# Masked projections of a four-layer kernel: the low half of the weights is multiplied with the high half of the activations only, in 64-row matmuls behind the whole matmuls of four groups

## The reference, cut to what matters

```python
xn = layernorm(gn(x), norm_w, norm_b)
left  = (xn @ w_left ) * m * sigmoid(xn @ w_lgate)   # m: mask of the token, layers 0 and 2
right = (xn @ w_right) * m * sigmoid(xn @ w_rgate)
out = einsum('bikh,bjkh->bijh', left, right)         # layer 0; the others alike
x = x + (layernorm(out, onorm_w, onorm_b) * sigmoid(xn @ w_ogate)) @ w_out
```

## Time and profile before

| | |
|---|---|
| median of 3 runs | 2098.76 us (2098.36 to 2103.34) |
| profiled execution, its own time | 2098.03 us |
| its span, first to last instruction | 2096.1 us |
| mean granted TensorE clock | 0.962 |
| busy: TensorE, VectorE, ScalarE, GpSimd | 90%, 81%, 76%, 29% |

### The profile page before, as it was taken

One profiled execution on the slowest core, in us unless ns is written; L12 is line 12 of the kernel. 1 busy time (PEld: TensorE's weight loads), 2 busy tenths in 40 slices (PEclk: granted clock), 3 DMA queues, 4 the chain that ended last, 5 costly groups with the idle time before them and its releaser, 6 DMA issues. The chain is left out here.

```text
span 2096.1 us, 44730 instructions
## 1 busy us (share of the span) xinstructions
PE 1876.4 (90%) x14492; PEld 1270.1 (61%) x14492; DVE 1687.9 (81%) x2690; ACT 1587.1 (76%) x2204; POOL 599.5 (29%) x574
## 2 busy tenths in 40 slices
PE   5698979789888999989989899999997889999998
PEld 4423959555422778865632598987552258877665
DVE  6799989989689868778959997978776987777654
ACT  3598969769899647658989885876888976666676
POOL 0001918265200000016500380742870000000755
PEclk8899989999999999999999999999999999999999
DMA  9599938289789838269969965927997994844997
GB/s 395 208 303 316 252 81 232 78 308 368 300 266 335 295 120 291 72 241 389 418 240 317 298 192 151 277 55 282 396 405 255 310 328 158 276 158 164 337 346 277
DMA packets 297397, 549.53 MB, mean 262 GB/s; under 512 B 14768, under 2 KB 170416, under 8 KB 273712
## 3 DMA queue, kind: packets, MB, share of 16 engines
q1 hardware_dynamic: 295680, 538.38, 74.3%
q10 hardware_dynamic: 1584, 9.51, 1.1%
HBM read 371.67 MB, written 176.16 MB: 261 GB/s over the span
## 5 line engine op out<-in xcount | busy, mean ns | idle before, releaser
L1609 POOL TENSOR_TENSOR LR<-LR,sum 128x2048 f32<-128x2048 f32 x30 | 136.6, 4553 | 513.2 <-DVE LR L1422 513.2
L1618 POOL TENSOR_TENSOR LR<-LR 128x512 f32<-128x512 f32 x96 | 140.6, 1483 | 482.4 <-DVE LR L1664 482.2
L677 PE MATMUL bank<-LR,kst 128*128 128x512 f32 x512 | 255.1, 621 | 8.5 <-ACT LR L699 6.3
L877 POOL TENSOR_TENSOR msgs<-sigs,mask_sb 128x256 f32<-128x256 f32 x192 | 129.8, 691 | 463.8 <-ACT sigs L851 460.4
L1512 PEld LDWEIGHTS bank<-kst,LR 128*128 128x128 f32 x1024 | 151.0, 192 | 109.7 <-issue 90.7
L1524 PE MATMUL bank<-LR,wog 128*128 128x512 f16 x768 | 211.7, 385 | 4.7 <-ACT msgs L1565 3.9
L677 PEld LDWEIGHTS bank<-LR,kst 128*128 128x128 f32 x512 | 88.1, 192 | 180.1 <-issue 173.7
L1019 PE MATMUL bank<-LR 128*128 128x256 f32 x768 | 170.9, 384 | 7.0 <-DVE LR L916 4.2
L1277 PE MATMUL bank<-LR 128*128 128x256 f32 x768 | 166.6, 379 | 7.0 <-DVE LR L916 4.2
L1512 PE MATMUL bank<-kst,LR 128*128 128x128 f32 x1024 | 159.4, 279 | 13.9 <-ACT sigs L1560 7.7
L1019 PEld LDWEIGHTS bank<-LR 128*128 128x128 f32 x768 | 147.4, 193 | 27.7 <-DVE LR L916 4.6
(11 more groups left out here) (227 smaller groups left out, 4800.5 us busy)
## 6 DMA issues: line engine op xcount, KB each, us to landing
LR<-XT SPq DMA_DIRECT2D x89, 1024.0 KB, 8.5
XT<-LR SPq DMA_DIRECT2D x47, 1024.0 KB, 8.8
kept<-XH SPq DMA_DIRECT2D x64, 512.0 KB, 5.7
LR<-XH SPq DMA_DIRECT2D x64, 512.0 KB, 6.8
kept<-XHA SPq DMA_DIRECT2D x64, 512.0 KB, 5.2
LR<-XHA SPq DMA_DIRECT2D x64, 512.0 KB, 5.9
OS<-kept SPq DMA_DIRECT2D x12, 2048.0 KB, 8.3
LR<-OS SPq DMA_DIRECT2D x48, 512.0 KB, 8.7
```

Source lines behind the costliest of these rows:

```text
L677: last = pe.matmul(banks[3][:, u * BANK:(u + 1) * BANK], K(K_MEAN), sq[t % 3][:, u * BANK:(u + 1) * BANK], start=True, stop=True)
L1609: pool.tensor_tensor(v, v, token(sum2, c, C), ALU.mult).then_inc(normalized.s, 1)
L1618: pool.tensor_tensor(by_b(x_of(c), q) if end else by_token_cols(x_of(c), q), by_token(gated[t % 4]), by_token_cols(xi[c % len(xi)], q), AL ...
```

## The change

`where` now gives groups in the order of `q` with the two sides next to each other, instead of all of side 0 and then all of side 1. A half of a chunk (four groups, `two` = 0 or 1) first gets its 16 whole matmuls with `whigh`, each group behind its own wait for a free bank. Then come its 16 `wlow` matmuls over 64 rows, alternating between the sides. The first two groups of the half are signalled at the end of the first eight of these, and the other two at the end of the last eight. The product of the low weights with the low activations is no longer formed. Every other engine keeps its code.

```diff
             def where(n, g):
-                return g // 4, 16 * n + 4 * (g % 4)
+                return g % 2, 16 * n + 4 * (g // 2)
...
                         if masked:
-                            for g in range(8):
-                                if g % 2 == 0:
-                                    norm_left(h, g // 2)
-                                pe.wait_ge(products_ready.s, products_ready.n + 32 * i + 8 * h + g - 7)
-                                for j in range(4):
-                                    for part, w in enumerate((whigh, wlow)):
-                                        last = pe.matmul(bank(g)[:, j * P:(j + 1) * P],
-                                                         tokens(h, g // 4, g % 4, j, slice(0, P)),
-                                                         w[:, half * P:(half + 1) * P], start=part == 0, stop=part == 1)
-                                last.then_inc(projected.s, 1)
+                            for two in range(2):
+                                for g in range(4 * two, 4 * two + 4):
+                                    if g % 2 == 0:
+                                        norm_left(h, g // 2)
+                                    pe.wait_ge(products_ready.s, products_ready.n + 32 * i + 8 * h + g - 7)
+                                    for j in range(4):
+                                        pe.matmul(bank(g)[:, j * P:(j + 1) * P],
+                                                  tokens(h, g % 2, g // 2, j, slice(0, P)),
+                                                  whigh[:, half * P:(half + 1) * P], start=j == 0, stop=False)
+                                for q in (2 * two, 2 * two + 1):
+                                    for s, j in sides_last:
+                                        rows = slice(C * s, C * s + C)
+                                        last = pe.matmul(bank(2 * q + s)[:, j * P:(j + 1) * P], tokens(h, s, q, j, rows),
+                                                         wlow[rows, half * P:(half + 1) * P], start=False, stop=j == 3)
+                                        if j == 3:
+                                            last.then_inc(projected.s, 1)
```

## The result

The changed kernel is slower. The first four runs gave a median of 2129.11 us (2121.01 to 2129.31), against 2099.61 for the kernel before: ratio 1.0117, interval 1.0098 to 1.0136. I had forecast 2110 us and a range up to 2125. The direction and the mechanism held; the size did not. A second series of the same kernel, next to 17 runs of the kernel before, gave 2120.83 us (2119.01 to 2124.76) against 2100.89, ratio 1.0095 with interval 1.0076 to 1.0113. So the change cost 29.5 us in the first series, outside my range, and 19.9 us in the second, inside it. The forecast of 10.8 us was about a half of the smaller of the two.

A forecast was written before the change was run, and what follows sets the result against it. TensorE's matmuls bound the kernel at 4.01 us per chunk; a 4.17 us ring would replace them. The four projections' +1.8, +4.7, +1.8 and +2.5 sum to +10.8 us, 2098.8 to about 2110, range 2100 to 2125.

The forecast's parts named there:

- the ring: Masked projections: each half-chunk passes TensorE, ScalarE, GpSimd and VectorE once per chunk without a buffer, 4.17 us against 4.01.
- TensorE's work on a chunk: Masked projections: whole and 64-row matmuls plus switches take TensorE 3.36 us per chunk, down 0.63.
- the floor of 3.80 us: Masked projections: VectorE needs 1.90 us per half-chunk, 3.80 per chunk, as read after a table load.
- the pairs that start together: 64-row matmuls of the two sides start together, a pair costing 0.055 us in layers without mask, taken as 0.062 here.
- steps 2 to 4 of the ring: From first whole matmul to sigmoid: whole matmuls 0.19, switch to narrow ones 0.15, first narrow start to sigmoid 0.47 us.
- step 2: On TensorE: four whole matmuls, first to last start, 3 x 0.0624 = 0.19 us.
- step 4: TensorE to ScalarE: first narrow matmul start to the sigmoid, 0.44 us plus 0.03 for strided tokens, 0.47 us.
- step 1: VectorE to TensorE: from group 3's product taken to the first whole matmul of that bank, 0.06 us.
- Step 5: ScalarE, GpSimd, VectorE: sigmoid of group 0 to the end of group 3's product, 3.30 us.
- the first rival: Masked projections: TensorE's relief counts, each chunk falls to VectorE's 3.80 us, giving 2089 us; chance 0.08.
- The rival of a clock that falls in the projections: TensorE's gaps lower its clock, TensorE's part of the turn grows by about 0.6 us, giving 2145 us; chance 0.02.
- the longer figure: Port wait of VectorE's mask to the end of GpSimd's record: 0.26 instead of 0.13 us, 4.30 us per chunk.

The follow-up runs named there:

- the order alone: Changed kernel with its second pass over all 128 rows again, so only the new matmul order stays: 2125.99 us, ratio 1.0111 to the kernel before.
- a ring over two banks: Changed kernel with the 64-row matmuls behind two groups' whole matmuls instead of four: 2113.42 us, ratio 1.0051 to the kernel before.
- the kernel before with the table ahead: Kernel before with the sigmoid table loaded ahead of the loop in the second projection: 2101.28 us, ratio 0.9993 to the kernel before.

## Why the prediction was right and wrong

**Right: the ring.** That the last bank of a half holds up all four, that this outlasts TensorE's work and VectorE's floor, and that the time rises for it, is shown from three sides: the order alone costs the same, a ring over two banks costs less in spite of more switches, and without the masks the same order wins. TensorE's work on a chunk was put too low, 3.36 us where the run without masks has 3.6. It did not decide, since both lie below the ring.

**Right: the floor of 3.80 us**, the pairs that start together, and no role for the loads in the steady pace. In the first profile one load was late: TensorE waited 1.2 us for `first_home` in the fifth chunk of the first projection, and that chunk took 6.22 us where it takes 4.40 in the second profile, which does not have this wait.

**Wrong: steps 2 to 4 of the ring, 0.81 us in the sum.** They measured 0.99 (0.24, 0.16 and 0.59, where the prediction has 0.19, 0.15 and 0.47), so product to sigmoid took 1.05 instead of 0.87. I had taken the switch and the signal from layers whose tokens lie side by side and allowed 0.03 for the stride in the pitch of the pairs. It is not the pitch that suffers. The first matmul after a wait and the first after a switch are followed after 0.11 us instead of 0.06, once in step 2 and once in step 4. That is 0.10 of the 0.18, and side by side 0.14 of it goes away. The restart could have been read from the kernel before, behind the very wait that step 1 uses:

```profile
333.68 0.28 PE L813 MATMUL bank<-whigh,kept 128*128 128x128 f16 x1
333.79 0.23 PE L813 MATMUL bank<-wlow,kept 128*128 128x128 f16 x1
```

Most of the rest stands between the last record of the first four pairs and the sigmoid: with tokens side by side it is still 0.52 us from the first narrow matmul to the sigmoid, where the layers without mask have 0.44. The changed kernel without the masks has 0.50 there with the same strides, against 0.59 with the masks. So up to 0.09 goes with the masks or with the wait for them on ScalarE, which that run replaced by another wait. Which of the two was not tested.

**Step 5 was 0.07 too long**, 3.23 instead of 3.30, and a turn of the loop adds about 0.15 to every fourth chunk, which I had left out. Together 4.32 on the mean of the fourth projection instead of 4.17, 0.15 more. Over 60 chunks that is 9 us, against 8.0 by which the projections of the second profile exceed the forecast in the table. (The prediction multiplies by 59 in its rivals, where its own terms add up to 58. With 58 the first rival's 2089 becomes 2085; the forecast does not use it.)

| projection | forecast | measured, second profile |
|---|---|---|
| first | +1.8 | 65.96 - 62.23 = +3.7 |
| second | +4.7 | 68.43 - 62.65 = +5.8, and 0.8 at its start |
| third | +1.8 | 65.97 - 62.20 = +3.8 |
| fourth | +2.5 | 64.83 - 60.10 = +4.7 |
| sum | +10.8 | +18.8 |

The start of the second is the time from its first matmul to the end of its first chunk, 9.17 us against 8.33 in the kernel before, so 0.8 where 0.9 was forecast; the other loads cost 1.3 to 1.4 where 1.28 was forecast. These two terms were right. Another 1.2 us stand ahead of that matmul, in the contraction, whose code is the same (41.92 us against 40.73, and 40.73 again in the kernel before with the table ahead); why is open. Together this is 20.0, which is the 19.9 of the medians of the second series; the two profiled executions differ by 22.8, so the agreement to a tenth is luck.

**The other 9 us of the first series** are a second step that failed: the prediction put the stretches whose code is the same at nothing. The first profile took 8.5 us more than the second. Of these 3.1 lie in the projections, for the most part in the first two, which hold the late load and stretches at a granted clock of 0.50 behind it and near a table load. And 5.6 lie between the second projection and the third, 799.9 us at a granted clock of 0.96 against 794.3 at 0.97 (796.1 at 0.97 in the kernel before). The rest are smaller differences of both signs. The ten runs of the changed kernel show the same link: five at a mean clock of 0.962 to 0.964 took 2119.0 to 2121.0 us, five at 0.957 to 0.959 took 2123.8 to 2129.3. The first series had three of its four runs at 0.957 or 0.958. The link is looser in other kernels: two runs of the changed kernel without the mask, both at 0.963, took 2069.96 and 2077.28. Whether the gaps of TensorE bring low-clock executions on is open. The order alone has such gaps as well, and all its runs lie at 0.963 to 0.965. The rival of a clock that falls in the projections did not come in: they are at 1.00 in most stretches, and the dips to 0.50 stand at starts and ends of stages, at a table load and behind the late load.

The range failed for these reasons together. It held the ring from 4.02 to 4.42, which contains 4.28 and 4.32, and it holds the 2120.83 of the second series. But the projections apart from the ring, and the clock outside of them, had no width of their own, and the 2129.11 of the first series lies above it.

**Pairs and the shared port.** The Trainium skill, page TensorE: Matmul & The Clock Gate, in the part on packing small matmuls, states the concurrency of matmuls on different row groups. It holds here with starts within 0.01 us, but it spoke for a gain that the order took away. The Trainium skill, page SBUF — State Buffer, section SBUF: two separate sides, states that whoever starts first holds the port pair for the whole instruction. Taken to the end of GpSimd's record this would have made the way back longer than 3.30 us. It measured 3.23, so the trace does not support the longer figure. The traces show by how much: in the second profile VectorE's mask takes a median of 0.15 us more than its free 0.41 in 48 cases in which it starts with 0.27 us of GpSimd's record left, and 0.48 more in 7 cases with 0.60 left. The wait ends about 0.12 us before the record does.

## What to carry to other kernels

When an order makes a signal wait for several buffers, add up the way round once, from the release of the last buffer to its next release, and compare it with each engine's work; the longest of these is the pace, and less work on an engine does not help when the ring is longer. Read the floor of engines that look full where the trace shows them catching up, as behind a table load. Take the price of a switch or a restart from rows with the same access pattern, or keep it as a bound: here the rows with other strides left the first part of the ring about 0.1 us short per turn, and there were 60 turns. Before you call a difference the price of an instruction, run the kernel without it: the chunks with a table load were 1.5 us longer than their neighbours, but 0.15 of it stayed when the load had gone.

## What the runs showed of the hardware

- After a wait or a switch between 128 and 64 rows, a matmul with strided weights (steps of 16 elements) is followed by the next after 0.11 us, one with weights side by side after 0.066 us (medians over the changed kernel and the same with tokens side by side). In a row the two pitches are 0.062 and 0.056. Where the second pass keeps 128 rows, no such step is seen at its start: 0.063 and 0.062.
- Pairs of 64-row matmuls on the two halves of the rows start within 0.01 us of each other with strided weights as well.
- VectorE's mask multiply takes 0.40 us of record when nothing is in its way, and mostly 0.41 to 0.56 at the changed kernel's pace, beside GpSimd's masks, in single cases up to 0.89. Its wait ends about 0.12 us before the end of GpSimd's record.
- A table load inside the loop takes 1.28 us in each iteration, though the table is the same, and costs 1.3 to 1.4 us in the ring and 0.6 us where eight independent banks can catch up.
- The mean granted clock of one execution varied from 0.957 to 0.964 over ten runs of the changed kernel in two series, and the time from 2119.0 to 2129.3 us.
